# Block transposes on VectorE, and the low part on GpSimd, for the probabilities of the looped attention groups

## The reference

```python
x = x + attn(layernorm(x), w_q, w_k, w_v, w_o)
x = x + xattn(ctx, ctx, layernorm(x))
x = x + ffn(layernorm(x), int4 gate, up and down weights with scales and zeros)

# attn, for each of 8 sequences of 128 positions, each of 8 key/value heads, each of its 4 query heads:
scores = q @ k.T * 128 ** -0.5           # 128 queries x 128 keys
scores = where(causal, scores, -inf)     # a key behind its query does not count
probs  = softmax(scores)
attn   = probs @ v                       # then all heads @ w_o
```

## Time and profile before

| | us |
|---|---|
| median of 3 runs | 760.26 (760.12 to 760.35) |
| profiled execution, its own time | 761.72 |
| span of its trace | 759.9 |
| start of the loop, first mask of the first looped group | 34.96 |
| one looped group, mask of its tile 0 to mask of the next group's tile 0 | 250.00 to 321.69 |
| behind the loop | 536.8 to 759.9 |

### The profile page before, as it was taken

How to read it: one execution, slowest core, us unless ns; L and a number is a source line. 1 busy time by engine, 2 the same in 40 slices (tenths; PEclk the granted TensorE clock), 3 DMA queues, 4 the chain that set the end, 5 groups by cost and what they waited for, 6 DMA issues and landing times.

```text
span 759.9 us, 11191 instructions
## 1 busy us (share of the span) xinstructions
PE 737.2 (97%) x3718; PEld 614.3 (81%) x3718; DVE 511.0 (67%) x685; ACT 384.4 (51%) x962; POOL 308.1 (41%) x317
## 2 busy tenths in 40 slices
PE   7999999999999999999999999999999979999994
PEld 6888888888888888888888888888887757888873
DVE  7557836864675567457736773676258878888887
ACT  4355436443563554265526543553456565656542
POOL 4452314322331332152304322422244644689885
PEclk9999999999999999999999999999999999999997
DMA  9412033202322040203023101302720002212102
GB/s 300 117 57 80 1 107 110 79 38 68 119 70 84 23 162 17 96 27 142 0 86 110 59 28 39 110 28 68 255 78 1 1 1 57 83 42 77 28 12 110
DMA packets 44351, 56.44 MB, mean 74 GB/s; under 512 B 7432, under 2 KB 26056, under 8 KB 44328
## 3 DMA queue, kind: packets, MB, share of 16 engines
q1 hardware_dynamic: 44328, 56.15, 22.7%
HBM read 45.26 MB, written 10.88 MB: 74 GB/s over the span
## 4 chain that ended last, share of the span: by engine, by line
PE 87%; DVE 5%; POOL 2%; issue 2%; ACT 2%; DMA 0%; POOLq 0%; ACTq 0%; DVEq 0%
PE psum L454 20%; PE psum L456 20%; PE psum L455 20%; PE psum L588 7%; PE psum L647 5%; PE psum L648 5%; PE psum L597 3%; PE psum L670 2%; PE psum L669 2%; DVE stats L1143 1%; PE psum L460 1%; PE psum L474 1%; ACT probs L859 1%; POOL o_sum L1103 1%; DVE xprobs L1252 1%
## 5 line engine op out<-in xcount | busy, mean ns | idle before, releaser
L1057 POOL TENSOR_TENSOR probs<-probs,rowinv 128x512 f32<-128x512 f32 x64 | 71.2, 1113 | 304.1 <-DVE rowinv L1332 304.1
L859 ACT ACTIVATE probs<-probs,negmax 128x128 f32<-128x128 f32 x256 | 99.8, 391 | 60.6 <-DVE negmax L1319 60.6
L454 PE MATMUL psum<-xt_hi,wq_hi 128*128 128x512 f32 x256 | 104.4, 408 | 0.0
L852 ACT CAST pt_hi<-psum 128x512 fp32r<-128x512 f32 x64 | 37.6, 587 | 128.2 <-PE psum L597 128.2
L454 PE MATMUL psum<-wo_hi,at_hi 128*128 128x512 f32 x256 | 100.3, 392 | 0.5 <-DVE at_lo L1352 0.5
L456 PE MATMUL psum<-xt_hi,wq_lo 128*128 128x512 f32 x256 | 100.2, 391 | 0.0
L455 PE MATMUL psum<-xt_lo,wq_hi 128*128 128x512 f32 x256 | 99.9, 390 | 0.0
L456 PE MATMUL psum<-wo_hi,at_lo 128*128 128x512 f32 x256 | 99.7, 389 | 0.0
L455 PE MATMUL psum<-wo_lo,at_hi 128*128 128x512 f32 x256 | 99.6, 389 | 0.0
L1352 DVE TENSOR_TENSOR at_lo<-psum,at_hi 128x512 fp32r<-128x512 f32 x64 | 44.1, 689 | 72.0 <-ACT at_hi L887 72.0
L764 ACT ACTIVATE qt<-psum 128x512 f32<-128x512 f32 x64 | 38.0, 594 | 75.8 <-PE psum L456 74.1
(11 more groups left out here) (145 smaller groups left out, 1628.1 us busy)
## 6 DMA issues: line engine op xcount, KB each, us to landing
wq_raw<-in_L_attn_w_q SPq DMA_DIRECT2D x8, 1024.0 KB, 5.5
wo_raw<-in_L_attn_w_o SPq DMA_DIRECT2D x8, 1024.0 KB, 7.7
unpacked_w<-u_q SPq DMA_DIRECT2D x8, 688.0 KB, 3.0
gw<-unpacked_w SPq DMA_DIRECT2D x20, 256.0 KB, 3.4
unpacked_w<-u_q SPq DMA_DIRECT2D x6, 512.0 KB, 2.6
u_q<-in_L_ffn_gate_qweight SPq DMA_DIRECT2D x8, 344.0 KB, 7.2
u_q<-in_L_ffn_up_qweight SPq DMA_DIRECT2D x8, 344.0 KB, 3.8
u_q<-in_L_ffn_down_qweight SPq DMA_DIRECT2D x10, 256.0 KB, 3.4
```

Of the source, the lines that this page charges most:

```text
L454: pe.matmul(dst, a_hi, b_hi, start=start, stop=False)
L859: e = act.activation(probs[:, t % 2, j, :], probs[:, t % 2, j, :], ACT.Exp, bias=negmax[:, t % 2, j:j + 1], accum_out=rowsum[:, t % 2, j:j ...
L1057: pool.tensor_tensor(probs[:, t % 2], probs[:, t % 2], rowinv[:, t % 2, :].unsqueeze(2).to_broadcast([P, HG, P]), ALU.mult).then_inc(prob_ ...
```

## The change

In the looped groups PE no longer turns the probabilities. DVE does, right behind the reciprocal of the same slot: `turn_probs(g, t)` waits for POOL's product (`prob_ready`) and for the low part of the tile before (`ptlo_ready`, which frees `pt`), then issues ten transposes. Each takes 32 queries x 4 heads x 32 keys out of `probs` and writes 32 keys x 4 heads x 32 queries of the new SBUF tile `pt` in one instruction on 32 partitions. Ten pairs of the 4 x 4 grid are needed, since blocks with all keys behind their queries stay zero; `pt` is cleared once, ahead of the loop. ACT casts `pt_hi` out of `pt` instead of PSUM, and POOL, not DVE, forms `pt_lo`, ahead of its product in each slot. The unpack steps move: one in each of slots 0 to 3, two in each of slots 8 and 9, all at the slot's end. The last group stays as it was.

```diff
+    QUAD = 32
+    UNPACK = {0: 1, 1: 1, 2: 1, 3: 1, 8: 2, 9: 2}
...
+            pt = sb("pt", [P, HG, P])
...
# PE
-                    if 1 <= t <= NB:
+                    if 1 <= t <= NB and not more:
                         u = t - 1
                         pe.wait_ge(prob_ready, step + u + 1)
                         pe.wait_ge(ptlo_ready, step + u + PRIME)
...
# ACT
-                        act.wait_ge(pt_done, step + u + 1 + PRIME)
+                        if more:
+                            act.wait_ge(pt_turned, step + u + 1)
+                        else:
+                            act.wait_ge(pt_done, u + 1 + PRIME)
                         act.wait_ge(pv_done, step + u + PRIME)
-                        act.copy(pt_hi[:], psum[:, BK_T, :].rearrange("p (a b) -> p a b", a=HG)
+                        act.copy(pt_hi[:], pt[:] if more else psum[:, BK_T, :].rearrange("p (a b) -> p a b", a=HG)
                                  ).then_inc(pthi_ready, 1)
...
# POOL
+                    if 1 <= t <= NB and more:
+                        pool.wait_ge(pthi_ready, step + t)
+                        pool.tensor_tensor(pt_lo[:], pt[:], pt_hi[:].bitcast(F32), ALU.subtract).then_inc(ptlo_ready, 1)
                     if t < NB:
                         pool.wait_ge(inv_ready, step + t + 1)
...
# DVE
+            def turn_probs(g, t):
+
+                dve.wait_ge(prob_ready, g * NB + t + 1)
+                dve.wait_ge(ptlo_ready, g * NB + t + PRIME)
+                for i in range(P // QUAD):
+                    for j in range(i + 1):
+                        queries, keys = slice(i * QUAD, (i + 1) * QUAD), slice(j * QUAD, (j + 1) * QUAD)
+                        turned = dve.transpose(pt[keys, :, queries], probs[queries, t % 2, :, keys])
+                turned.then_inc(pt_turned, 1)
...
-                    if 1 <= t <= NB:
+                    if 1 <= t <= NB and not more:
                         u = t - 1
                         dve.wait_ge(pthi_ready, step + u + 1)
                         dve.tensor_tensor(pt_lo[:], psum[:, BK_T, :].rearrange("p (a b) -> p a b", a=HG),
...
+                    if t < NB and more:
+                        turn_probs(g, t)
                     if t in TURN_V and (more or TURN_V[t] == 1):
...
-                    if more and t < 2:
-                        unpack_step(g, t)
...
-                    elif 2 <= t < 2 * STEPS:
-                        unpack_step(g, t)
...
+                    else:
+                        for i in range(UNPACK.get(t, 0)):
+                            unpack_step(g, sum(UNPACK.get(s, 0) for s in range(t)) + i)
...
+            dve.memset(pt[:], 0.0).then_inc(consts_dve, 1)
```

More of the change, by code:

```diff
@@ L214, in decoder_kernel @@
         prob_ready = sem("prob_ready")
+        pt_turned = sem("pt_turned")
         pt_done = sem("pt_done")
@@ L1313, in group @@
                         dve.wait_ge(score_done, step + t + 1 + PRIME)
-                        dve.wait_ge(pt_done, step + t - 1 + PRIME)
+                        if not more:
+                            dve.wait_ge(pt_done, t - 1 + PRIME)
                         dve.tensor_tensor(probs[:, r], psum[:, BK_S, :].rearrange("p (a b) -> p a b", a=HG),
@@ L1362, in group @@
                         third_second(t - AT_NORM3)
-                    elif 2 <= t < 2 * STEPS:
-                        unpack_step(g, t)
-            dve.wait_ge(consts_dve, 1)
+                    else:
+                        for i in range(UNPACK.get(t, 0)):
+                            unpack_step(g, sum(UNPACK.get(s, 0) for s in range(t)) + i)
+            dve.memset(pt[:], 0.0).then_inc(consts_dve, 1)
+            dve.wait_ge(consts_dve, 2)
             with dve.Fori(0, LAST) as g:
```

## The result

The changed kernel takes 850.45 us (median of 4 runs, 848.42 to 853.33) where the kernel before takes 760.19 in the same comparison: a ratio of 1.119, 95% interval 1.1149 to 1.1232, slower by 90.3 us.

A forecast was written before the change was run, and what follows sets the result against it. PE bounded the kernel before; DVE's serial chain would bound it after. A looped group goes from 71.7 to 83.8 us, 12.1 more, times seven is 85, so 760.3 becomes 845 us, range 783 to 878.

The forecast's parts named there:

- the tail: From tile 7's mask to the next group's mask: 19.6 us, about the same as before (19.63).
- T: Time of each of DVE's ten transposes per tile: 0.31 us, 3.1 us a tile; DVE is the bound above 0.17.
- the upper of the two bounds: Step of a transpose that waits for the last one's end: 0.31 to 0.33 us, against 0.20 if they overlap.
- Rivals 1 to 3: Transposes overlap (chance 0.15), are slower than 0.36 us (918 us, 0.10), or read two columns a cycle (744 us, 0.04).
- Rival 1: DVE's transposes overlap, 0.20 to 0.25 us each: 783 us in all, or 811 at 0.25; chance 0.15.
- inner range: The forecast itself, each transpose taking 0.27 to 0.36 us: 818 to 873 us, chance 0.66.
- the outer one: The whole range, 783 to 878 us, from transposes of 0.20 us up to the forecast's upper end.
- The slots: DVE's mask-to-mask times in slots 0 to 6 of a looped group, 64.2 us to the mask of tile 7.
- rival 4: PE's clock falls as PE idles some 19% of a group; in one slot of each group, 884 us; chance 0.04.
- the clock still full: Expected sign in the changed kernel's trace: PE's clock granted in full, with PE busy near 81% of a group.
- the forecast's 68.2: Looped group's time in us if PE stays the bound, 71.7 less 3.5 for the transposes PE is spared.
- rival 3: Faster than before: DVE's transposes read two columns a cycle, about 0.13 us each, group 69.4, 744 us; chance 0.04.

The follow-up runs named there:

- e1: Changed kernel with every transpose reading and writing the same 32 partitions, three partition switches instead of nine, probabilities not turned rightly: 802.95 us.
- e3: Changed kernel with one unpack step in each of slots 0 to 7, all at the slot's end: 888.48 us.
- e5: Changed kernel with the same ten correct transposes in another order, the input switching partitions eight times and the output three times: 851.13 us.
- e4: Changed kernel with small matmuls on PE ahead of its wait for the low part, in slots 4 to 8: 843.93 us.
- e8: Kernel before the change, with only the unpack steps moved to the changed kernel's places: 783.18 us.
- e2: Changed kernel with one transpose for ten, all waits kept, probabilities not turned: 765.24 us.

## Why the prediction was right, and where its terms were off

**The direction and the size.** 850.45 against 845 forecast, in the range. The bound moved from PE to the serial chain on DVE, which the timeline shows (mask to mask with no wait for PE), and which e1 and e3 confirm from both sides: a shorter link shortens slots 1 to 6 and the tail (slot 0 alone is held by POOL's `wo_lo`), a longer one lengthens its slot, while DVE as a whole is busy 68% of the group.

**T.** Forecast 0.31, measured 0.315 (ten in 3.15). The reason for taking the upper of the two bounds, the switch of partitions, is shown by e1 and e5. Rivals 1 to 3 fall with it: the nine steps of the change lie between 0.312 and 0.321. Rival 1's step exists, but only where the partitions stay, and e1 with six of nine such steps lies at 803, in its range.

That T came out to 0.005 us is partly luck. The forecast added a length of 0.28 and 0.03 from the end to the next start; measured are 0.302 and 0.014, two errors that nearly cancel. The prediction also says that nine of the ten switch the output group. By the blocks' order eight of the nine steps do, and the ninth switches the input alone; the reading stands, as either is enough. The figure of 311 ns that it takes from the Trainium skill, VectorE: DVE Perf Modes, section The three transpose paths, is one for bf16 and 128 partitions; here, float32 on 32 partitions, it was 302 ns. And the lower end of its inner range does not follow from its own formula: T = 0.27 gives 823, not 818 (0.36 gives 873), and no working is shown for the 878 of the outer one. Nothing hangs on either end.

**The slots.** Forecast 9.0, 11.1, 9.1, 9.8, 8.2, 8.2, 8.8; measured 8.66, 10.96, 9.02, 9.74, 8.24, 8.24, 8.83. Only slot 0 is off by more than 0.15: its unpack step lasts 1.01, not 1.4. The steps of the other three last 2.20, 0.87 and 1.58 against 2.3, 0.9 and 1.6, and POOL's low part pays in slots 2 and 3 (1.90 and 2.62 instead of 1.29), as forecast. The waits were there as described: PE stands at PV for `pt_lo`, 48 times.

**The term that was mis-sized is the tail,** "19.6, about the same as before". Its steps hold where the clock does: 7.60 to the last transpose, 2.05 to PV, 19.7 in all. But in five of seven groups the heads of tile 6 then run for 3 us at PE's lower clock: +1.6 each, 8.1 us in all in the profiled execution. This is rival 4 on a small scale, to which I gave a whole slot and a chance of 0.04, and "the clock still full" was wrong: 0.96 in the group. The reading that misled me was the earlier trace rows: a mean busy share of 77% with a full clock says nothing on one idle stretch of 1.8 us in one piece. That the fall is the cause of these 8 us is shown by e4: with the gap filled all seven tails are at 19.7. PE's busy share came to 87% of a group, not 81%, and not because of the tail: the group without a fall there has it too (72.5 of 83.4). At most 1.7 us of the 4.3 over the forecast's 68.2 are matmuls at the lower clock in slot 2 (3.4 us at that level); for the rest, the profile lets each matmul ahead of an idle stretch end later than its step (0.39 against 0.23), which was not added up.

**The remainder.** The forecast is 12.1 x 7 = 84.7. A group without the fall is 83.41 against 83.8, 2.7 less in seven; the first group's slot 0 (9.22) adds 0.6; outside the loop the difference is 0.7. Together with the falls: 84.7 - 2.7 + 8.1 + 0.6 + 0.7 = 91.4, measured 91.6; the 0.2 left is rounding (71.7 for 71.67). Behind the loop 221.7 us passed, 223 forecast.

**A step that held only by its cover.** I costed the moved unpack steps by their length on DVE's chain, and that was right for this kernel. That e8 loses 23 us shows what hid the rest: the ten transposes fill the time in which DVE waited for `at_hi`. In the change `at_lo` follows them with no wait; in e2 and e8 slot 1's step stands behind that wait and meets `wo_lo`. So "if PE stays the bound, a group takes 68.2" could not have come true with these places for the steps, and rival 3 was priced too well: even with one transpose the kernel is at 765, not under 744.

**What stays open.** Why PE's clock falls after 1.8 us idle in five tails and not after the same 1.8 us in the two others (and in e8 after 1.84 us in four groups of seven) was not tried. Nor was the low part left on DVE with only the transposes moved, so what its way over ACT and POOL costs by itself is not known; with one transpose left, the rest of the change together comes to 5 us over before (e2). The 2.3 us ahead of the loop were only seen to vary.

## What to carry to other kernels

Before moving work to an engine that looks idle, write out its chain for one iteration, waits included; the iteration can't be shorter than that chain, whatever the busy share says. If the work must move, put it inside one of the waits, a stage later if need be (the same ten transposes stand in a kernel 90 us over before when they are ahead of the next mask, and in one 2 us under it when they are inside the wait for Exp, 8 us once two stalls there were shortened), and look at what used to fill that wait before taking it out. Order small VectorE instructions so that consecutive ones start at the same partitions on both sides.

## What the runs showed of the hardware

- A VectorE transpose of 32 partitions x 128 float32 columns lasts 302 ns when its input or its output starts at other partitions than the one before, and it starts only 0.014 us behind that one's end (nine such steps of 0.312 to 0.321 us in the change). Without a switch it lasts 257 ns and starts 0.19 us after the last one's start, 0.235 if that one had switched (e1).
- PE's granted clock fell to its lower level after single idle stretches of 1.8 us (five of seven in the change, three of seven in e5, four of seven in e8), not after others of the same length, and twelve matmuls of 512 columns behind one took 4.34 us instead of 2.73. Small matmuls in the gap prevented it in all seven tails.
- A two-source VectorE instruction beside a GpSimd one that started 0.05 us ahead of it lasted 2.70 instead of 1.67, and the two GpSimd ones 3.87 together instead of 2.55. The Trainium skill, SBUF — State Buffer, section SBUF: two separate sides, describes a port pair for which the two engines wait on each other for whole instructions; these lengths agree with waiting, on both sides.
- A one-source VectorE step on 128x1376 that starts while GpSimd forms `wo_lo` (1.29 us) ended 0.73 us behind that one's end, whether it had started 0.28 or 1.02 us behind its start: it lasted 1.75 in e1 and 1.01 in the change.
